# Projections and setup products spread between cross attention units, with a tanh gate and the final attention inside the feed-forward, in a transformer block with a second attention layer, on one core

## The chip, the cores and the metric

The kernel runs on 1 core of one Trainium2 chip, as one launch. The metric is the device time of that launch in microseconds, the median of a few runs. Its engines are TensorE (PE in the profile; PEld is its weight load), VectorE (DVE), ScalarE (ACT), GpSimd (POOL) and SyncE (SP, which here only issues DMAs).

## The reference

Input `x` is [2, 1024, 256], a context is [2, 77, 256]. Everything is fp32.

```
x  = x + attention1(ln1(x), ln1(x))          # 16 heads of 16, 1024 keys
x  = x + attention2(ln2(x), context)         # 16 heads of 16, 77 keys
h  = ln3(x) @ Wff1 + bff1                    # [., 2048]
lin, g = split(h)
x  = x + (lin * (g * sigmoid(1.702 * g))) @ Wff2 + bff2
# second layer: one head over the whole width of 256, 77 keys
Q, K, V = x Wq^T + bq, c Wk^T + bk, c Wv^T + bv
out = softmax(Q K^T / 16) V Wfc^T + bfc
x  = norm_w * rms_normalize(out + x)
```

The kernel never forms Q: it makes `g1 = Wq K^T`, `cb` (the part of the scores that comes from `bq`) and `vw = V Wfc^T + bfc` from the context and the weights once. These nine small products (two for K, two for V, two for `g1`, one for `cb`, two for `vw`) are called the setup products below.

## The kernel before

The program is written out by hand: each engine has its own stream, and semaphores join them. An engine runs its stream strictly in order, so that the place of a piece in the text is its place in time. Tokens are handled in 4 blocks of 512 (block 0 and 1 are batch 0), each of 4 tiles of 128; heads in 8 groups of 4 (groups 0 to 3 are batch 0). The stages:

- **Projections.** Block by block, layer norm, a transpose on PE (`turn`, L657), projections of q and k in two fp16 parts (`project`, L671; ACT makes the high part at L1142, DVE the remainder at L1489), which go to DRAM and come back in the layout that the score matmuls want. The keys' score maxima of group 0 begin here (`scores` L704, reduced by DVE in `reduce_tile`, L1497): 24 tiles of them before the first attention step. Between these tiles PE makes the products of the context (`setup`, L788), among them the nine setup products, which ACT copies out (L1202, L1204).
- **Self attention.** 8 groups of 16 steps; a step has four score matmuls (L856), four exponentials on ACT (L1246), the weighting (L868), and two tiles of maxima for the next group on DVE.
- **After self attention, batch 1.** `chain(0, 1)` is a generator of 17 pieces on each engine: two turns of the attended values, eight output products (L829) with the residual add (L1589) and layer norm on DVE, and for each of the blocks 2 and 3 a turn of the normalized rows (L657) and two projections to q of the cross attention (L671), and a last empty piece. `AHEAD` pieces run first, then pieces stand between the first tiles of cross scores (`FIRST_S2`, `scores_2`, L946), and the last three stand in cross group 0 (`pieces`).
- **Cross attention.** 8 groups of 8 units (`cross_unit`): a score matmul (L957), an exponential (L1304), and by unit number also a tile of maxima for the group after next (L946, reduced at L1686), the turn of the maxima (L982), the weighting (L965) and the turn of the result (L976). `chain(1, 0)`, the 12 pieces after cross attention of batch 0, stands in groups 5, 6 and 7.
- **Feed-forward.** 32 chunks (4 blocks of 8): `widen` (12 matmuls, L1033 to L1035, first the gate's bank, then the linear one), the gate on ACT with its bias (L1359), the product on DVE (`hidden`, L1734), a split in a high and low part (L1349 ACT, L1740 DVE), and three chunks later `narrow` (12 matmuls, L1048 to L1050). `chain(1, 1)` stands in the first eight chunks. For blocks 0 to 2 the turn of the finished rows and the scores of the final attention (L1063) follow in a later block.
- **Final attention.** After the last chunk: exponentials by tile with their sum (L1378), turns (L1072), copies (L1383), weighting (L1081), the residual (L1760), sums of squares (L1391), the root by 13 tiny DVE instructions a block (`root_steps`, L1447 to L1455), scaling on ACT (L1397) and on POOL (L614), for the last block on DVE (L1802), and stores.

```
TAIL = (1, 1, 1, 1, 1, 2, 1, 2, 1, 2, 2, 2)
AHEAD, FIRST_S2 = 6, (0, 1, 0, 1, 0, 1, 0, 1) * 2
def pieces(G, n):
    if G == 0:
        return 1 if n in (1, 3, 5) else 0
    return 1 if G >= GROUPS - 3 and n % 2 == 0 else 0
```

## Time and profile before

| | |
|---|---|
| median of 3 runs | 765.85 us (764.49 to 768.3) |
| the profiled execution, its time | 763.57 us |
| its span, first to last instruction | 761.1 us |
| mean granted TensorE clock | 0.943 |
| busy share of the span: PE, DVE, ACT, POOL | 90%, 72%, 66%, 9% |
| 512 exponentials of self attention on ACT | 312.8 us |

Times within the span count from its first instruction. The PEclk column of a stretch is the granted clock as a share of full speed: 1.00 is 2.4 GHz and 0.50 is 1.2 GHz. A matmul's busy time includes its way through the array, so the pace of a stream of matmuls is read from one start to the next.

### The profile page before, as it was taken

Reading aid. Unit: us, or ns where it says so; the run is one execution under the profiler, and the core shown is the slowest. Engines: PE = TensorE matmul, PEld = TensorE weight load, DVE = VectorE, ACT = ScalarE, POOL = GpSimd, SP = SyncE. Lnnn points to the kernel's source line nnn. Section 1 sums busy time; section 2 is a strip of 40 time slices with the busy share of each in tenths; the row PEclk is TensorE's granted clock in tenths of the full one; section 3 lists DMA queues with packets and bytes.
Section 4 is the critical chain, followed back from the end, with each engine's and each line's share of the span. In section 5 each row is a group of like instructions: output and inputs, shape, how many; then the busy total and the mean of one; then the engine's idle time right before and its main releaser. Section 6 shows DMA issues by size and latency. Waiting matters only on the chain.

```text
span 761.1 us, 11110 instructions
## 1 busy us (share of the span) xinstructions
PE 684.0 (90%) x4072; PEld 326.7 (43%) x4072; DVE 546.9 (72%) x954; ACT 501.5 (66%) x902; POOL 72.1 (9%) x85
## 2 busy tenths in 40 slices
PE   4989899999999999999999975899989999999981
PEld 2644422222222222222223342333547888888871
DVE  6678999999999999999973557544475954343367
ACT  2542499999999999999998731655664343233274
POOL 2080800000000000000000205100020110000004
PEclk9999999999999999999999997955788999999995
DMA  9456350202020100001000021211000000000003
GB/s 295 180 189 229 92 191 7 65 1 70 1 71 1 44 28 4 27 1 29 1 1 0 28 81 35 66 42 34 2 1 1 1 1 1 1 1 1 1 0 111
DMA packets 35113, 36.87 MB, mean 48 GB/s; under 512 B 6132, under 2 KB 28276, under 8 KB 34804
## 3 DMA queue, kind: packets, MB, share of 16 engines
q1 hardware_dynamic: 33904, 35.87, 14.8%
q8 instruction: 32, 0.52, 0.3%
q0 software_dynamic: 1024, 0.24, 0.3%
q14 instruction: 21, 0.17, 0.1%
q10 hardware_dynamic: 132, 0.07, 0.0%
HBM read 23.09 MB, written 12.74 MB: 47 GB/s over the span
## 4 chain that ended last, share of the span: by engine, by line
PE 70%; ACT 14%; DVE 10%; issue 5%; POOL 1%; ACTq 0%; DVEq 0%; POOLq 0%
PE ps L868 16%; PE ps L856 12%; ACT probs L1246 8%; PE ps L671 6%; PE ps L1033 4%; PE ps L1034 4%; PE ps L1035 4%; PE ps L829 3%; PE ps L965 3%; PE ps L657 3%; PE ps L704 2%; PE ps L957 2%; PE ps L976 2%; PE ps L1049 2%; PE ps L679 2%
## 5 line engine op out<-in xcount | busy, mean ns | idle before, releaser
L1246 ACT ACTIVATE probs<-ps,unfit 128x512 f32<-128x512 f32 x512 | 312.8, 693 | 21.5 <-PE ps L856 15.3
L1497 DVE TENSOR_REDUCE mm<-ps 128x2 f32<-128x1024 f32 x256 | 301.0, 1219 | 17.1 <-PE ps L704 9.6
L856 PE MATMUL ps<-stack 50*128 50x512 f16 x512 | 147.6, 384 | 11.6 <-ACT probs L1246 0.8
L868 PE MATMUL ps<-probs,v 128*32 128x512 f32 x1024 | 136.4, 604 | 2.7 <-ACT outT L1251 2.7
L856 PEld LDWEIGHTS ps<-stack 50*128 50x128 f16 x512 | 36.4, 93 | 191.1 <-ACT probs L1246 185.1
L704 PE MATMUL ps<-stack 48*128 48x512 f16 x512 | 105.6, 381 | 6.2 <-ACT mT L1191 4.5
L1359 ACT ACTIVATE early<-ps,cols 128x512 f32<-128x512 f32 x32 | 22.0, 687 | 88.4 <-PE ps L1035 88.4
L585 POOL TENSOR_TENSOR x<-x,rows 128x1024 f32<-128x1024 f32 x12 | 28.1, 2354 | 493.0 <-DVE tok L1478 492.9
L1734 DVE SCALAR_TENSOR_TENSOR hid<-ps,cols,early 128x512 f32<-128x512 f32 x32 | 24.0, 751 | 69.8 <-PE ps L1035 65.9
L1304 ACT ACTIVATE probs<-ps,unfit 96x512 f32<-96x512 f32 x64 | 42.3, 680 | 28.7 <-PE ps L957 28.5
L1033 PE MATMUL ps<-x_hi,wff_hi 128*128 128x512 f32 x128 | 52.0, 406 | 0.0
L1034 PE MATMUL ps<-x_lo,wff_hi 128*128 128x512 f32 x128 | 50.9, 398 | 0.0
L1035 PE MATMUL ps<-x_hi,wff_lo 128*128 128x512 f32 x128 | 50.4, 394 | 0.0
L1686 DVE TENSOR_REDUCE mm<-ps 128x8 f32<-128x616 f32 x32 | 25.5, 797 | 27.9 <-PE ps L946 27.8
L704 PEld LDWEIGHTS ps<-stack 48*128 48x128 f16 x512 | 25.7, 94 | 35.6 <-DVE mm L1497 10.4
L868 PEld LDWEIGHTS ps<-probs,v 128*32 128x32 f32 x1024 | 20.6, 107 | 37.3 <-issue 30.2
L1048 PE MATMUL ps<-wff_hi,hid_hi 128*128 128x256 f32 x128 | 36.5, 285 | 0.0
L1049 PE MATMUL ps<-wff_lo,hid_hi 128*128 128x256 f32 x128 | 36.1, 282 | 0.0
L829 PE MATMUL ps<-wo,wkv 128*128 128x256 f32 x128 | 33.6, 394 | 2.6 <-ACT wkv L1128 1.6
L1050 PE MATMUL ps<-wff_hi,hid_lo 128*128 128x256 f32 x128 | 35.8, 280 | 0.0
L1589 DVE TENSOR_TENSOR x<-ps,x 128x256 f32<-128x256 f32 x48 | 19.0, 418 | 23.3 <-PE ps L829 20.9
L1133 ACT ACTIVATE xT<-ps,cols 128x512 f32<-128x512 f32 x24 | 17.7, 778 | 25.1 <-PE ps L657 24.7
(164 smaller groups left out, 888.2 us busy)
## 6 DMA issues: line engine op xcount, KB each, us to landing
v_groups<-early SPq DMA_DIRECT2D x8, 512.0 KB, 3.1
stack<-q_parts SPq DMA_DIRECT2D x64, 64.0 KB, 2.0
v<-v_groups SPq DMA_DIRECT2D x8, 512.0 KB, 4.1
x<-in_x SPq DMA_DIRECT2D x4, 512.0 KB, 7.6
q_parts<-probs SPq DMA_DIRECT2D x8, 256.0 KB, 3.9
k_parts<-probs SPq DMA_DIRECT2D x8, 256.0 KB, 2.1
stack<-k_parts SPq DMA_DIRECT2D x16, 128.0 KB, 2.6
stack<-q_parts SPq DMA_DIRECT2D x64, 32.0 KB, 1.9
```

The lines of the kernel that those rows point to most:

```text
L671: mm_ = eng.matmul(ps[:, proj_bank(u), 0:n], w[:, c, P * o:P * o + P], src[:, c, c0:c0 + n], start=(c == 0), stop=(c == NC - 1))
L704: mm_ = eng.matmul(ps[:, 2 * s_slot(G, j, i) + tile, :], qs[rows_i, slot, half, q, P * t:P * t + P], stack[rows_i, SLOTS + slot, q, BLK * ...
L829: mm_ = eng.matmul(ps[:, out_bank(k), 0:D], attT[i // TPB][:, c, P * t:P * t + P], w[:, c, :], start=(c == 0), stop=(c == NC - 1))
L856: eng.matmul(ps[:, st_bank(n), :], stack[rows_of(tile, KROWS), SLOTS + slot, q, P * kc:P * kc + P], qs[rows_of(tile, KROWS), slot, half, q ...
L868: mm_ = eng.matmul(ps[32 * h:32 * h + 32, PV, :], v1[:, G % 2, kc, 32 * h:32 * h + 32], probs[:, k % 2, h, :], start=(kc == 0), stop=(kc = ...
L1033: eng.matmul(ps[:, bank, :], wh, xh[:, c, :], start=(c == 0), stop=False)
L1034: eng.matmul(ps[:, bank, :], wh, xl[:, c, :], start=False, stop=False)
L1035: mm_ = eng.matmul(ps[:, bank, :], wl, xh[:, c, :], start=False, stop=(c == NC - 1))
L1049: eng.matmul(out, hh, w2l, start=False, stop=False)
L1246: eng.activation(probs[:, k % 2, HEADS[h], :], ps[:, st_bank(n), :], ACT.Exp, scale=unfit[:, 0:1]).then_inc(exp_done, 1)
L1304: eng.activation(probs[0:CTXP, half, HEADS[h], :], ps[0:CTXP, ST + h % 2, :], ACT.Exp, scale=unfit[0:CTXP, 1:2]).then_inc(exp_done, 1)
L1497: eng.tensor_reduce(dst, ps[:, 2 * slot:2 * slot + 2, :], AX.X, ALU.max).then_inc(s_red, 1)
```

## The change

1. **Setup products.** The nine leave the projections stage. A generator `final_setup` on PE and DVE puts them in units (2,1), (2,3), (2,5), (3,0), (3,2), (3,4), (3,6), (4,1), (4,3) (group, unit) of cross attention. DVE copies them out, no longer ACT. 22 and no longer 24 tiles of maxima (`FIRST_TILES = 11` pairs) come before the first attention step; the last two stand inside that step. The turn of the first maxima stands after the 18th tile.
2. **Projections.** The four pieces of `chain(0, 1)` in the second half of `FIRST_S2`, and the three of group 0, now stand in groups 0 and 1, one to every second unit; `chain(1, 0)` begins one unit of work earlier, at the end of group 4. The fp16 parts of the cross q go to six slots in the space of the used keys, since their old place still holds weights. SP stores block 2's parts, loads group 4's first half, stores block 3's, and then loads the second half.
3. **Gate.** `g * sigmoid(1.702 g)` is computed as `(tanh(0.851 g) + 1) * (0.5 g)`: two activations on ACT (`Tanh` and `Identity`) and one more DVE instruction (`gated_half`) a chunk.
4. **Final attention.** For blocks 0 to 2 all of it is in the feed-forward's chunks; exponentials are one instruction a block after a subtraction of the maximum on DVE, and ACT and POOL no longer scale. Of block 2 the weighting and what follows is still at the end. For block 3 it goes by pairs of tiles: the last four chunks are narrowed tile by tile, so that the first two tiles finish earlier. The sum of the exponentials for block 3 comes from a column of ones in `vw`.

The diff's core:

```diff
-        AHEAD, FIRST_S2 = 6, (0, 1, 0, 1, 0, 1, 0, 1) * 2
+        AHEAD, FIRST_S2 = 6, (0, 1, 0, 1, 0, 1, 0, 1) + (0,) * 8
...
-            if G == 0:
-                return 1 if n in (1, 3, 5) else 0
-            return 1 if G >= GROUPS - 3 and n % 2 == 0 else 0
+            if G < len(PIECES_1):
+                return PIECES_1[G][n]
+            return PIECES_2[G - GROUPS // 2][n] if G >= GROUPS // 2 else 0
+
+        PIECES_1 = ((1, 0, 1, 0, 1, 0, 1, 0), (1, 0, 1, 0, 1, 0, 0, 0))
+        PIECES_2 = ((0, 0, 0, 0, 0, 0, 0, 1), (1, 0, 1, 0, 1, 0, 1, 0), (1, 0, 1, 0, 1, 0, 1, 0), (1, 0, 1, 0, 1, 0, 0, 0))
+        SETUP_UNITS = ((2, 1), (2, 3), (2, 5), (3, 0), (3, 2), (3, 4), (3, 6), (4, 1), (4, 3))
...
+            while first_scores:
+                tile_of_scores()
+                if len(first_scores) == 2 * FIRST_TILES - 18:
+                    eng.wait_ge(su_done, SETUP_1)
+                    eng.wait_ge(m_step, 3)
+                    eng.matmul(ps[0:96, MISC, 0:P], mpart[:, 0, :], identh[:, :], start=True, stop=True).then_inc(m_turned, 1)
...
                     cross_unit(G, n)
-                    advance(after_self if G == 0 else after_cross, pieces(G, n))
+                    if (G, n) in SETUP_UNITS:
+                        next(fillers)
+                    advance(after_self if G < GPB else after_cross, pieces(G, n))
...
-                eng.activation(gate[:, n % 2, :], ps[:, GATE, :], ACT.Gelu_apprx_sigmoid,
-                               bias=cols[:, i:i + 1]).then_inc(gate_done, 1)
+                eng.activation(gate[:, n % 2, :], ps[:, GATE, :], ACT.Tanh, scale=GELU / 2, bias=gate_cols[:, 0, f:f + 1])
+                eng.activation(half_gate[:, n % 2, :], ps[:, GATE, :], ACT.Identity, scale=0.5,
+                               bias=gate_cols[:, 1, f:f + 1]).then_inc(gate_done, 1)
...
+            def gated_half(n):
+                eng.wait_ge(gate_done, n + 1)
+                g = gate[:, n % 2, :]
+                eng.scalar_tensor_tensor(out=g, in0=g, scalar=1.0, in1=half_gate[:, n % 2, :], op0=ALU.add, op1=ALU.mult).then_inc(gated, 1)
...
+                if i == 4:
+                    l1_turn(blk)
+                if i == 5:
+                    l1_weigh(blk)
...
+            narrow_last(LAST_CHUNKS[0:3], (0, 1, 2))
+            l1_weigh(last - 1)
+            narrow_last(LAST_CHUNKS[3:4], (0, 1, 2))
+            narrow_last(LAST_CHUNKS[0:2], (3,))
+            last_turn(0)
+            narrow_last(LAST_CHUNKS[2:4], (3,))
+            last_scores(0)
+            last_turn(1)
+            last_scores(1)
+            last_turn_probs(0)
+            last_weigh(0)
+            last_turn_probs(1)
+            last_weigh(1)
```

How the streams move, at three places (line numbers are each kernel's own).

PE at the start of cross attention, before: L946 is a tile of cross maxima, L982 the turn of the maxima, L671 a projection, L657 a turn of rows, L957 the first unit's score matmul.

```order
L657 MATMUL ps<-ident,tok 128x128 x8
L946 MATMUL ps<-k,stack 128x78 x8
L982 MATMUL ps<-identh,mpart 96x128
L671 MATMUL ps<-xT,wq 128x512 x2
L946 MATMUL ps<-k,stack 128x78 x8
L671 MATMUL ps<-xT,wq 128x512 x2
L946 MATMUL ps<-k,stack 128x78 x8
L657 MATMUL ps<-ident,tok 128x128 x8
L957 MATMUL ps<-stack,k 96x512
```

The same place in the changed kernel, where L992 is the tile of maxima, L1028 its turn, L1003 the unit's score matmul, L678 a turn and L692 a projection.

```order
L992 MATMUL ps<-k,stack 128x78 x16
L1028 MATMUL ps<-identh,mpart 96x128
L992 MATMUL ps<-k,stack 128x78 x16
L1003 MATMUL ps<-stack,k 96x512
L992 MATMUL ps<-k,stack 128x78 x8
L678 MATMUL ps<-ident,tok 128x128 x8
L1003 MATMUL ps<-stack,k 96x512 x2
L992 MATMUL ps<-k,stack 128x78 x8
L1028 MATMUL ps<-identh,mpart 96x128
L692 MATMUL ps<-xT,wq 128x512 x2
```

Two turns and two projections no longer stand before the first unit, but behind it.

DVE in a chunk in the middle of the feed-forward, before:

```order
L1734 SCALAR_TENSOR_TENSOR hid<-ps,cols,early 128x512
L1740 TENSOR_TENSOR hid_lo<-hid,hid_hi 128x512
L1677 TENSOR_TENSOR x_lo<-xT,x_hi_56 128x2x512
L1734 SCALAR_TENSOR_TENSOR hid<-ps,cols,early 128x512
L1740 TENSOR_TENSOR hid_lo<-hid,hid_hi 128x512
```

and in the changed kernel, where L1867 is `gated_half`, L1877 `hidden`, L1883 the low part, L1560 and L1563 steps of the root, and L1922 the last scaling of a finished block:

```order
L1883 TENSOR_TENSOR hid_lo<-hid,hid_hi 128x512
L1560 TENSOR_TENSOR ms<-rms 128x4
L1560 TENSOR_TENSOR ms<-ms,half_ms 128x4
L1563 SCALAR_TENSOR_TENSOR rms<-ms,rms 128x4
L1560 TENSOR_TENSOR ms<-rms 128x4
L1560 TENSOR_TENSOR ms<-ms,half_ms 128x4
L1563 SCALAR_TENSOR_TENSOR rms<-ms,rms 128x4
L1867 SCALAR_TENSOR_TENSOR early<-early 128x512
L1877 SCALAR_TENSOR_TENSOR hid<-ps,cols,early 128x512
L1811 TENSOR_TENSOR x_lo<-xT,x_hi_56 128x2x512
L1922 SCALAR_TENSOR_TENSOR x<-x,rms,rows 128x256 x4
L1883 TENSOR_TENSOR hid_lo<-hid,hid_hi 128x512
```

A chunk has one long DVE instruction more, and in some chunks the work of the final attention.

PE from the end of the last chunk on, before (L1072 turns the probabilities, L657 the rows, L1081 weights, L1063 makes scores):

```order
L1050 MATMUL ps<-wff_hi,hid_lo 128x256
L1072 MATMUL ps<-ident,probs 77x128 x8
L657 MATMUL ps<-ident,x 128x128 x8
L1081 MATMUL ps<-vw,p1T 128x256 x4
L1063 MATMUL ps<-g,xT 128x77 x8
L1072 MATMUL ps<-ident,probs 77x128 x4
L1081 MATMUL ps<-vw,p1T 128x256 x8
L1072 MATMUL ps<-ident,probs 77x128 x4
L1081 MATMUL ps<-vw,p1T 128x256 x4
```

and now (L1157 turns rows, L1167 makes scores, L1176 turns probabilities, L1185 weights):

```order
L1095 MATMUL ps<-wff_hi,hid_lo 128x256
L1167 MATMUL ps<-g,xT 128x77 x4
L1157 MATMUL ps<-ident,x 128x128 x4
L1167 MATMUL ps<-g,xT 128x77 x4
L1176 MATMUL ps<-ident,probs 77x128 x2
L1185 MATMUL ps<-vw,p1T 128x257 x2
L1176 MATMUL ps<-ident,probs 77x128 x2
L1185 MATMUL ps<-vw,p1T 128x257 x2
```

What was three blocks and a fourth is now the fourth alone, in two halves.

## Rows read from the trace of the kernel before

**Rows 1.** The page: granted TensorE clock in 40 slices; the gate's group
```profile
PEclk9999999999999999999999997955788999999995
...
L1359 ACT ACTIVATE early<-ps,cols 128x512 f32<-128x512 f32 x32 | 22.0, 687 | 88.4 <-PE ps L1035 88.4
```

**Rows 2.** Busy time by stretch: us of each engine (instructions), PEclk, DMA share, GB/s
```profile
462.00:473.00 11.00, 6.11 (x23) 3.10 (x23) 7.05 (x24) 1.82 (x3) 5.47 (x5) 0.53 0.01 3
473.00:493.00 20.00, 16.90 (x135) 7.41 (x135) 11.90 (x19) 13.51 (x24) 5.07 (x6) 1.00 0.20 64
493.00:541.00 48.00, 45.89 (x266) 19.23 (x267) 18.94 (x39) 25.29 (x45) 0.00 (x0) 0.50 0.11 31
541.00:565.00 24.00, 22.52 (x137) 11.25 (x133) 17.31 (x62) 17.25 (x30) 2.36 (x1) 1.00 0.01 2
...
592.00:606.00 14.00, 13.14 (x75) 11.36 (x74) 13.41 (x37) 4.40 (x7) 2.37 (x1) 1.00 0.01 2
606.00:723.60 117.60, 117.60 (x704) 103.73 (x703) 50.45 (x96) 39.42 (x64) 2.40 (x1) 1.00 0.00 1
```

**Rows 3.** Timeline, end of the projections: start, us, engine, line, [idle before]
```profile
79.33 8.00 DVE L1497 TENSOR_REDUCE mm<-ps 128x2 f32<-128x1024 f32 x7
...
90.01 4.15 ACT L1246 ACTIVATE probs<-ps,unfit 128x512 f32<-128x512 f32 x7 [0.56 <-PE ps L856]
...
90.16 9.44 DVE L1497 TENSOR_REDUCE mm<-ps 128x2 f32<-128x1024 f32 x8 [1.45 <-PE ps L704]
```

**Rows 4.** Timeline, end of the stage between the attentions
```profile
466.68 1.38 DVE L1478 TENSOR_SCALAR tok<-x,mv,rstd 128x256 f32<-128x256 f32 x4
...
469.33 3.73 PE L671 MATMUL ps<-xT,wq 128*128 128x512 f32 x4
...
473.23 1.98 PE L671 MATMUL ps<-xT,wq 128*128 128x512 f32 x4
...
477.98 0.41 PE L957 MATMUL ps<-stack,k 50*96 50x512 f16 x1
```

**Rows 5.** Chain of waits, two setup products: start, us, what
```profile
84.42 0.72 PE ps L788 x4
...
87.44 1.61 PE ps L788 x6
```

**Rows 6.** Timeline of PE, cross attention: weightings, turns of maxima, one turn of rows
```profile
484.62 1.06 PE L965 MATMUL ps<-probs,v 96*32 96x512 f32 x8
...
492.99 1.54 PE L965 MATMUL ps<-probs,v 96*32 96x512 f32 x8
...
501.15 0.34 PE L982 MATMUL ps<-identh,mpart 128*96 128x128 f16 x1
...
524.94 0.34 PE L982 MATMUL ps<-identh,mpart 128*96 128x128 f16 x1
...
538.67 1.91 PE L657 MATMUL ps<-ident,tok 128*128 128x128 f32 x8
```

**Rows 7.** Timeline of DVE, one chunk of block 2
```profile
655.59 0.75 DVE L1734 SCALAR_TENSOR_TENSOR hid<-ps,cols,early 128x512 f32<-128x512 f32 x1 [2.84 <-PE ps L1035]
656.26 0.68 DVE L1740 TENSOR_TENSOR hid_lo<-hid,hid_hi 128x512 fp32r<-128x512 f32 x1
```

**Rows 8.** Groups by line after 723.6: busy us, mean ns, idle before
```profile
L1391 ACT ACTIVATE sq<-x 128x256 f32<-128x256 f32 x16 | 6.6, 413 | 1.1
...
L1391 ACT ACTIVATION_READ_ACCUMULATOR sq<-x 128x1 f32 x16 | 3.0, 187 | 0.0
```

**Rows 9.** Timeline after the last chunk's widening
```profile
729.19 1.04 PE L1072 MATMUL ps<-ident,probs 128*77 128x128 f32 x8
...
743.59 0.65 DVE L1452 TENSOR_TENSOR ms<-ms,half_ms 128x4 f32<-128x4 f32 x1
...
755.81 0.16 DVE L1455 SCALAR_TENSOR_TENSOR rms<-ms,rms 128x4 f32<-128x4 f32 x1
756.01 1.67 DVE L1802 SCALAR_TENSOR_TENSOR x<-x,rms,rows 128x256 f32<-128x256 f32 x4
```

More of the change, by code:

```diff
@@ L787, in setup @@
                 for i, (lhs, rhs) in enumerate(terms):
-                    mm_ = eng.matmul(ps[0:m, 6 + k % 2, 0:n], lhs, rhs, start=(i == 0), stop=(i == len(terms) - 1))
+                    mm_ = eng.matmul(ps[0:m, bank, 0:n], lhs, rhs, start=(i == 0), stop=(i == len(terms) - 1))
                 mm_.then_inc(su_full, 1)
-                tile_of_scores()
-            eng.wait_ge(w_in["wl1"], 64)
             cut = [slice(CTX * b, CTX * b + CTX) for b in range(B)]
             for b in range(B):
-                setup(CTX, D, [(ctxT[:, c, cut[b]], wkv2[:, c, D:2 * D]) for c in range(NC)])
@@ L1084, in _, with last_weigh @@
+            def last_weigh(p):
+                eng.wait_ge(l_pT, last + p + 1)
+                if p == 0:
+                    eng.wait_ge(l_y, TPB * last)
+                for t in range(2 * p, 2 * p + 2):
+                    eng.matmul(ps[:, LAST_W[p] + t % 2, 0:D + 1], p1T[0:CTXP, last, P * t:P * t + P],
+                               vw[0:CTXP, last // 2, :], start=True, stop=True).then_inc(l_pv, 1)
             eng.wait_ge(exp_done, 72 * GROUPS)
@@ L1417, in _ @@
+            hid_high(FC * BLOCKS - 1)
+            last_copy(0)
+            l1_squares(last - 1, (0, 1))
+            last_copy(1)
+            l1_squares(last - 1, (2, 3))
+            last_exps(0)
+            last_exps(1)
+            last_turn_copy(0)
+            last_turn_copy(1)
+            l1_squares(last, range(TPB))
         @block.vector
@@ L1632, in step @@
                     attended(2 * G, 2 * turn_slot(G, k))
+                if G == 0 and k == 0:
+                    for i in range(2):
+                        reduce_tile(G, FIRST_TILES, i)
                 if lead < GROUPS:
@@ new lines, in _, with last_max, last_residual @@
+            last = BLOCKS - 1
+            def last_max(p):
+                tiles = slice(2 * p, 2 * p + 2)
+                less_max(last + p, s1[:, last, tiles, :], ps[:, LAST_S[p], 0:2 * CTX].rearrange("p (t n) -> p t n", t=2),
+                         m1[:, last, tiles], [P, 2, CTX], last // 2)
+            def last_residual(p):
+                n, bank = TPB * last + 2 * p, LAST_W[p]
+                eng.wait_ge(l_pv, n + 2)
+                link(eng.reciprocal(r1[:, last, 2 * p:2 * p + 2], ps[:, bank:bank + 2, D]))
+                for t in range(2):
+                    eng.scalar_tensor_tensor(out=x[:, n + t, :], in0=ps[:, bank + t, 0:D], scalar=r1[:, last, 2 * p + t:2 * p + t + 1],
+                                             in1=x[:, n + t, :], op0=ALU.mult, op1=ALU.add).then_inc(l_y, 1)
@@ new lines, in steps_of @@
+            def steps_of(chain, n):
+                for _ in range(n):
+                    next(chain, None)
+            after_cross = chain(1, 1)
+            root = iter(())
+            for n in range(FC * BLOCKS):
+                blk, i = final_step(n)
+                if n >= 1:
+                    hid_low(n - 1)
+                if i == 0 and blk >= 1:
+                    root = l1_root(blk - 1)
+                    steps_of(root, 6)
+                if i == 1 and blk >= 1:
+                    steps_of(root, 7)
+                if i == 4:
+                    l1_sum(blk)
+                gated_half(n)
+                hidden(n)
@@ new lines, in _ @@
+            hid_low(FC * BLOCKS - 1)
+            l1_residual(last - 1, (0, 1))
+            for t in range(2):
+                add(2, TPB * last + t)
+            l1_residual(last - 1, (2, 3))
+            for t in range(2, TPB):
+                add(2, TPB * last + t)
+            root = l1_root(last - 1)
+            last_max(0)
+            steps_of(root, 6)
+            last_max(1)
+            steps_of(root, 7)
+            last_residual(0)
+            l1_scale(last - 1, (0, 1), l_out)
@@ L1807 @@
+            last_residual(1)
+            l1_scale(last - 1, (2, 3), l_out)
+            for _ in l1_root(last):
+                pass
+            l1_scale(last, range(TPB), l_last)
 def kernel(**inputs):
```

479 lines of the change are left out of this document (266 added, 213 removed).

## The prediction

> **What bounds the kernel now.** I read the page's slices first: PE is busy nearly everywhere, so a stage is mostly worth what its PE stream lasts, but the granted clock has a dip in the third quarter [rows 1]. The windows by stage come next [rows 2]. In 462 to 473 PE is busy 6.1 of 11 us at a clock of 0.53: the engines wait there. In 493 to 541 PE is busy 45.9 of 48 us, all of it at 0.50 (1.2 GHz): 48 us of cross attention at the lower level, though PE hardly rests. From 606 to 723.6 PE has no gap. After 723.6, where the last chunk's widening ends, another 37.4 us pass to the end of the span: a tail of short instructions that wait for each other [rows 8, 9]. The timelines of the four places show what ends each wait.
>
> At the start of self attention DVE decides: its reductions of maxima run one behind the other from 79.33, at 1.14 us each (8.00 for 7), while the first exponential starts at 90.01, and DVE itself then idles 1.45 us before the 25th tile [rows 3]. Between the attentions the layer norm on DVE ends at 468.06 (466.68 + 1.38), then two projections and a turn pass through PE, ACT and DVE before the first unit's matmul at 477.98 [rows 4].
>
> **The change, part by part.**
>
> *Start of self attention.* Nine products leave PE and 24 tiles become 22. The last reduction of 22 ends 2 x 1.14 = 2.3 us earlier, so the first exponential could start 4 to 5 us sooner, but every step then wants two tiles from a DVE that still owes two. DVE loses its idle 1.45 us, and ACT, which paces the plain steps, makes up the rest only if PE's order lets it. Bounds: 0 (DVE-paced, and later slack eats it) and 5 (ACT keeps its whole lead). I take **2.5 us** gained, a little above DVE's own 1.6 to 2.3, being nearest to it.
>
> *Before the first cross unit.* What is left behind the layer norm at 468.06 is three tiles of maxima, for each of which I allow 1.2 us through PE and DVE, and the turn of the maxima with its DMA. That ends near 472, and the unit starts there, not at 477.98 [rows 4]: **6.0 us** gained. The clock had fallen before 473 [rows 2] and PE now does less there, so the units begin at the lower level. Before, it was back at 473, after the projection of 3.73 us at 469.33. Now a turn stands behind unit 0 and a projection behind unit 2; I charge **3.0 us** lost (about 6 us of PE work at half speed until then), with bounds of 1 and 8.
>
> *Work that moves into the units.* Two turns at 1.0 and two projections at 2.0 [rows 4, 9] are 6.0 us; seven setup products at 0.9 and two at 1.6 [rows 5] are 9.5 us. In all **15.5 us** of PE work, on a PE that is the bound here. ACT is busy 25.3 of 48 us and DVE 18.9 in that stretch [rows 2], so DVE's nine copies (about 0.35 us each) hide. ACT loses them.
>
> *The clock in the units.* Two groups from one turn of maxima to that of two groups later take 23.8 us at the lower level, 11.9 a group [rows 6]. At the full level a group without pieces between, from one weighting to the third, takes 8.4 us (484.62 to 492.99) with some 1.2 us of gaps on PE, so 7.2 of work; a piece in the gaps fills them partly, I allow 0.5 a group. Four groups ran at the lower level. If the clock stays at full, they give back 4 x (11.9 - 7.2) = 18.8, less 2.0 for what gaps stay: **16.8 us** gained. Why it should stay: before, it fell in group 1, after the last projection and with only narrow work behind it, and was back in group 5 behind two turns (1.91 us at 538.67) [rows 6]; from 541 to 565, with a piece in every second unit, it stood at 1.00 [rows 2]. The new order puts a piece in nearly every second unit of groups 0 to 7. The longest stretches without one are the end of group 1 and three units of group 4, shorter than what it survived before it fell.
>
> The Trainium skill's page TensorE: Matmul & The Clock Gate, in the section on the clock gate ("What's actually happening"), says that the gate follows how busy PE has recently been. By that, units at 96% busy would have been at the full level, and pieces that raise 96% to 100% would change nothing; here the trace disagrees with its 48 us at 0.50. By that rule the 16.8 us would not come from the pieces, and the outcome would be the first rival's.
>
> *Feed-forward.* A chunk lasts 4.19 us on PE (DVE: 2.84 idle, then 0.67 and 0.68) [rows 7]. DVE gets a third instruction of 0.68 to 0.75, so 2.1 of 4.19; ACT a second activation, about 0.6, so 1.9. The path gate bank, tanh 0.69 (as the gate's activation now [rows 1]), identity 0.6, `gated_half` 0.7, `hidden` 0.75 and semaphores is 3.0 us, and the linear bank is wanted again 4.2 us after the gate's end: 1 us to spare, so nothing, if it stays there. In the first eight chunks DVE is busy 13.4 of 14 us with layer norm [rows 2]; there 0.7 us more in three or four chunks lands on the path: **2.5 us** lost, bounds 0 and 6. Final attention inside the chunks puts two turns of 0.45 and two weightings of 1.0 on PE: **2.9 us** lost. DVE's share of it, per block 4 scalings and 4 residuals at 0.42, 13 root steps at 0.2 and the maxima, is 9 us on some 20 us of idle in eight chunks; hidden. The setup of tanh needs no load of a table between exponentials and gate, which I book at nothing at the start.
>
> *Tail.* Before: 37.4 us. After, from the last widening, at the pace of the last 48 matmuls of `narrow`, from 723.6 to 729.19 [rows 9], 0.117 each: a turn 0.45, 36 of them 4.2, weighting 1.0, six more 0.7: 6.4. Turn and copy of the first pair of tiles, 1.3: 7.7. Scores 0.9, second turn 0.5, its copy behind two squares (0.60 each [rows 8]): 9.9; scores: 10.9. DVE: six root steps wait for the squares of block 2 (11.1): 12.4, maxima 1.0: 13.4. Exponential 0.45, copy 0.5, weighting 0.9: 15.2. Two residual pairs of 1.1 and two scalings of 0.85: 19.3. Root 13 x 0.2 (0.16 busy [rows 9]): 21.9. Four scalings 1.7 [rows 9]: 23.6. The output's transfer took 3.4 us before (757.7 to the end): 27.0. Part of it is that POOL is silent: beside POOL's scaling a root step took 0.65 us, without it 0.16 [rows 9]. **10.4 us** gained, bounds 7 and 13.
>
> *Sum*: 2.5 + 6.0 - 3.0 - 15.5 + 16.8 - 2.5 - 2.9 + 10.4 = 11.8 us gained. The profiled execution took 763.57 us (span 761.1), so the forecast is 751.8, rounded to **752 us**. The median of the runs shown, 765.85, lies 2.3 us above that execution; I do not add it.
>
> **The rivals.**
>
> *The clock stays at the lower level among the pieces.* The units' own work does not hold the clock, and small pieces (0.9 us in two units) may not either. Then each of four groups costs 11.9 as before plus its pieces at half speed: the 16.8 us are not gained and the 15.5 us double, so 32 us worse than the forecast: 784 us, slower. For it: the half level lasted 48 us with PE 96% busy [rows 2], and the stage now begins low. Against it: two turns ended it. A group at the lower level costs 4.2 + 3.9 = 8.1 us, so it decides from about two groups on (11.8 + 3.8 lost); one such group gives 760.
>
> *DVE and ACT become the bound of the chunks.* If the spare 1 us is gone, because a wait is longer than the busy times or pieces of final attention stand before `gated_half`, each chunk slips. At 0.4 us in 24 chunks that is 10 us: 762 us, no change. For it: four engines' hops in series where there were three; DVE's 96% in the first block [rows 2]. Against it: 2.84 us of idle DVE in each chunk [rows 7].
>
> *A transfer is late.* Group 4's second half of q is loaded only after block 3's projections, now in group 1; the store, its landing and four loads take some 8 us from there, and group 4's maxima want it in the middle of group 2, about as late. Two or three us, 755; in the range.
>
> **How the numbers follow.** A measurement of this kernel tells differences over 0.5%, 3.8 us. Forecast with the clock held, 744 to 758 with its terms' bounds: 0.72. The clock lost for about one group, or the late transfer with it, 757 to 762: 0.12. The chunks slip, 759 to 767: 0.08, half of it over 762. The clock lost for two groups or more, 768 to 785: 0.08. The range 744 to 762 leaves 0.12 at the upper side and some at the lower. Faster 0.87, same 0.06, slower 0.07.
>
> **What would show it.** Right: a granted clock of 1.00 from soon after the first unit to the feed-forward; the first unit's matmul some 8 us earlier; units of about 10 to 11 us a group with PE over 90% busy; PE without gaps in blocks 1 to 3; 27 us from the last widening to the end. Wrong: 0.50 in groups 2 to 4; PE waiting for DVE's product or ACT's gate in most chunks; the first exponential earlier but group 1 of self attention not; a tail where ACT's squares or DVE's root are preceded by idle time over 2 us.

## The result, and the profile after

| | before | changed kernel |
|---|---|---|
| median | 765.84 us (764.49 to 768.3, 4 runs) | 756.86 us (756.29 to 758.41, 4 runs) |
| profiled execution, its time / span | 763.57 / 761.1 us | 756.29 / 754.5 us |
| mean granted clock | 0.943 | 0.954 |

The ratio is 0.9892 (95% interval 0.9852 to 0.9932): faster by about 1.1%, over the 0.5% that a measurement of this kernel can tell. The forecast was 752 us, 4.9 us below the median. Compared as gains, the medians lie 9.0 us apart and the two profiled spans 6.6 us, where 11.8 us were forecast.

The kernel before has a wide spread of its own: of 19 later executions of it, five took 757.9 to 758.5 us at a mean granted clock of 0.949 and the others 761.1 to 768.1 us at 0.931 to 0.943, so that its best executions, of which no trace was kept, come close to the changed kernel's 756.3 to 758.4.

The granted clock on the page, in slices of 18.9 us:

```profile
PEclk9999699999999999999999997899968999999996
```

The dip of [rows 1] is nearly gone from the third quarter; what is left lies at its two ends, and a new dip stands in the fifth slice, at the start of self attention. The windows that answer to [rows 2] (busy time of each engine, granted clock, DMA share, GB/s):

```profile
462.00:473.00 11.00, 2.94 (x36) 1.85 (x37) 8.53 (x28) 0.93 (x2) 5.46 (x5) 0.50 0.01 3
473.00:493.00 20.00, 18.34 (x115) 8.40 (x113) 8.39 (x15) 13.68 (x25) 4.38 (x5) 0.89 0.16 51
493.00:541.00 48.00, 45.52 (x378) 23.73 (x378) 29.74 (x74) 31.89 (x58) 0.00 (x0) 1.00 0.13 37
...
552.00:570.00 18.00, 14.74 (x51) 8.10 (x52) 7.44 (x20) 8.68 (x14) 2.35 (x1) 0.53 0.01 1
```

From 493 to 541 PE is as busy as before (45.5 of 48 us against 45.9), but at 1.00 and not at 0.50. With more work in them the units are shorter. But the level falls again before the feed-forward: 0.53 from 552 to 570.

To place the rest, I cut both executions at the same instructions. On ACT these are copies of turned maxima (L1300, L1391), on DVE the first, ninth and last `hidden` (L1877). For the changed kernel, from the timeline:

```profile
100.50 0.25 ACT L1300 ACTIVATE mT<-ps 32x128 f16<-32x128 f32 x1
...
468.75 0.27 ACT L1391 ACTIVATE mT<-ps 64x128 f16<-64x128 f32 x1 [22.41 <-PE ps L1028]
479.60 0.26 ACT L1391 ACTIVATE mT<-ps 64x128 f16<-64x128 f32 x1
541.53 0.26 ACT L1391 ACTIVATE mT<-ps 64x128 f16<-64x128 f32 x1
...
570.36 0.75 DVE L1877 SCALAR_TENSOR_TENSOR hid<-ps,cols,early 128x512 f32<-128x512 f32 x1
618.71 0.75 DVE L1877 SCALAR_TENSOR_TENSOR hid<-ps,cols,early 128x512 f32<-128x512 f32 x1
727.45 0.75 DVE L1877 SCALAR_TENSOR_TENSOR hid<-ps,cols,early 128x512 f32<-128x512 f32 x1
```

The differences of these starts, and of the same instructions in every other kernel of this study, make one table (us; the last column is the span's end less the last `hidden`):

| kernel | start to A | A to B | B to C | C to D | D to E | E to chunk 0 | 0 to 8 | 8 to 31 | tail |
|---|---|---|---|---|---|---|---|---|---|
| before | 103.1 | 296.8 | 69.6 | 13.3 | 68.7 | 26.4 | 41.4 | 104.3 | 37.4 |
| changed | 100.5 | 296.9 | 71.3 | 10.9 | 61.9 | 28.8 | 48.4 | 108.7 | 27.0 |
| e1 tanh alone | 103.0 | 297.0 | 69.7 | 13.2 | 73.3 | 26.5 | 48.3 | 104.4 | 36.2 |
| e2 spread alone | 102.7 | 297.0 | 69.6 | 10.8 | 67.9 | 29.2 | 42.0 | 104.3 | 37.4 |
| e3 no gated_half | 100.5 | 296.9 | 69.7 | 10.2 | 61.9 | 28.5 | 43.3 | 108.7 | 27.5 |
| e4 setup back | 100.8 | 296.9 | 71.3 | 10.9 | 67.9 | 29.2 | 46.4 | 108.8 | 27.0 |
| e5 fill start | 101.1 | 296.9 | 69.7 | 11.5 | 61.9 | 29.1 | 48.3 | 108.8 | 27.0 |
| e6 fill cross | 103.3 | 296.9 | 76.4 | 9.8 | 61.9 | 28.8 | 48.1 | 108.8 | 27.0 |
| e7 old gate first | 101.5 | 296.9 | 69.7 | 11.0 | 61.9 | 28.9 | 43.3 | 108.8 | 26.0 |
| e8 w1 early | 103.6 | 296.9 | 69.7 | 11.0 | 62.2 | 28.8 | 44.5 | 108.8 | 27.0 |
| e9 POOL in four | 104.0 | 296.9 | 68.4 | 10.0 | 61.9 | 28.8 | 47.3 | 108.8 | 27.0 |
| e10 all three | 104.2 | 296.9 | 68.4 | 10.0 | 62.2 | 28.0 | 41.5 | 108.8 | 27.0 |
| e11 and order | 100.5 | 296.9 | 68.4 | 10.8 | 62.2 | 28.7 | 41.9 | 108.8 | 27.0 |
| e12 half fill | 103.7 | 297.0 | 69.5 | 11.0 | 61.9 | 28.9 | 48.3 | 108.8 | 27.0 |

A and B are the second and the sixteenth copy, in the steady part of self attention; C, D and E belong to cross groups 0, 1 and 7.

Three things in it are no part of the change: they differ between executions of the same instructions. I call them draws.

- **The first column.** The changed kernel, e3, e6 to e8 and e12 have the same streams up to A and reach it between 100.5 and 103.7 us (e9 to e11, which differ there by POOL's addition alone, between 100.5 and 104.2). The first projection, at 14 us, runs at one clock level or the other: it took 1.96 us at 13.96 in the changed kernel and 3.75 at 14.04 in the kernel before, and e1, e6, e8 to e10 and e12 drew 3.75 again. A part of the rest goes with how long the lower level then lasts behind 79 us: to 92 in the changed kernel, to 95 in e7, whose A is at 101.5.
- **B to C.** The changed kernel's clock was 0.64 from 432 to 436, while e3, the same program up to the feed-forward, stood at 1.00 there. This costs 1.7 us (71.3 against the 69.6 or 69.7 of seven other kernels; e4 drew it too).
- **The first block.** In the changed kernel the clock is at 0.50 from 610.6 to 614.0 us. The eighth chunk, from `hidden` to `hidden`, takes 6.5 us; in e4, with the same chunks and the clock at 1.00, it takes 4.9. e1, e5, e6, e9 and e12 have such a stretch as well, the other kernels have none.

The last one matters most, since it lies in the stage where the forecast went wrong. Whole first block (chunk 0 to 8), of the kernel before, the changed one, e4 and e10; columns as in the windows above:

```profile
578.02:619.41 41.39, 39.79 (x215) 33.84 (x215) 31.43 (x78) 18.56 (x31) 4.77 (x2) 1.00 0.00 1
...
570.36:618.71 48.35, 43.34 (x228) 36.35 (x227) 37.18 (x87) 23.32 (x38) 5.74 (x2) 0.96 0.00 1
...
577.02:623.40 46.38, 41.69 (x228) 34.94 (x227) 37.17 (x87) 23.21 (x38) 5.73 (x2) 1.00 0.00 1
...
569.79:611.30 41.51, 40.77 (x228) 35.18 (x227) 27.49 (x75) 16.82 (x26) 6.94 (x8) 1.00 0.00 1
```

The eight intervals between one `hidden` and the next (us):

| kernel | 1 | 2 | 3 | 4 | 5 | 6 | 7 | 8 |
|---|---|---|---|---|---|---|---|---|
| before | 3.1 | 5.5 | 4.5 | 7.5 | 6.1 | 7.1 | 3.2 | 4.3 |
| changed | 4.4 | 5.5 | 4.9 | 10.3 | 5.5 | 7.9 | 3.4 | 6.5 |
| e4 setup back | 4.4 | 5.5 | 4.5 | 10.3 | 5.5 | 7.9 | 3.4 | 4.9 |
| e3 no gated_half | 3.8 | 5.6 | 4.8 | 9.5 | 4.7 | 7.1 | 2.9 | 4.9 |
| e7 old gate first | 3.7 | 5.5 | 4.5 | 9.5 | 4.7 | 7.1 | 2.8 | 5.5 |
| e8 w1 early | 4.3 | 5.5 | 4.5 | 9.7 | 4.9 | 7.3 | 3.4 | 4.9 |
| e10 all three | 3.7 | 5.5 | 4.5 | 7.5 | 4.5 | 6.7 | 3.4 | 5.8 |

### The profile page after: what moved, and what is told of

Same layout as the page of the kernel before. It is cut to its first block and busy times, and to the rows that moved or that the text cites. A ratio compares the mean times of both kernels' runs of the same rounds, so it can differ in the third digit from the quotient of the medians.

```text
span 754.5 us, 11157 instructions
## 1 busy us (share of the span) xinstructions
PE 671.8 (89%) x4072; PEld 321.6 (43%) x4072; DVE 574.1 (76%) x1014; ACT 508.9 (67%) x887; POOL 65.0 (9%) x74
## 5 line engine op out<-in xcount | busy, mean ns | idle before, releaser
L894 PE MATMUL ps<-stack 50*128 50x512 f16 x512 | 149.2, 389 | 10.8 <-ACT probs L1336 0.4
L725 PE MATMUL ps<-stack 48*128 48x512 f16 x512 | 107.8, 390 | 10.2 <-DVE mm L1605 5.2
L612 POOL TENSOR_TENSOR x<-x,rows 128x1024 f32<-128x1024 f32 x12 | 29.1, 2438 | 491.1 <-DVE tok L1586 491.0
L1867 DVE SCALAR_TENSOR_TENSOR early<-early 128x512 f32<-128x512 f32 x32 | 22.1, 691 | 34.4 <-ACT early L1453 34.4
L1452 ACT ACTIVATE early<-ps,gate_cols 128x512 f32<-128x512 f32 x32 | 22.0, 688 | 37.7 <-PE ps L1084 37.7
L1444 ACT ACTIVATE hid_hi<-hid 128x512 fp32r<-128x512 f32 x32 | 20.2, 632 | 39.0 <-DVE hid L1877 39.0
L1093 PE MATMUL ps<-wff_hi,hid_hi 128*128 128x256 f32 x128 | 38.1, 298 | 0.0
L1094 PE MATMUL ps<-wff_lo,hid_hi 128*128 128x256 f32 x128 | 36.2, 283 | 0.0
L1820 DVE TENSOR_REDUCE mm<-ps 128x8 f32<-128x616 f32 x32 | 25.5, 797 | 12.1 <-PE ps L992 11.5
```

What stands on the lines that cost most here:

```text
L725: mm_ = eng.matmul(ps[:, 2 * s_slot(G, j, i) + tile, :], qs[rows_i, slot, half, q, P * t:P * t + P], stack[rows_i, SLOTS + slot, q, BLK * ...
L894: eng.matmul(ps[:, st_bank(n), :], stack[rows_of(tile, KROWS), SLOTS + slot, q, P * kc:P * kc + P], qs[rows_of(tile, KROWS), slot, half, q ...
L1093: eng.matmul(out, hh, w2h, start=(f == 0), stop=False)
L1094: eng.matmul(out, hh, w2l, start=False, stop=False)
```

## The experiments

Before them my theory was: the spread pieces, the nine small products above all, hold the clock in the units; and the missing 5 us lie in the first feed-forward block, where DVE was full and I priced `gated_half` too low. Rivals: the clock would hold without the products; the block is late for another reason. The changed kernel was timed in the first series alone, so a difference to its 756.86 us is one between series; the kernel before had medians of 765.8, 765.8, 766.4 and 765.7 us in the four series.

**e1, the tanh gate alone.** The kernel before, with

```diff
-                eng.activation(gate[:, n % 2, :], ps[:, GATE, :], ACT.Gelu_apprx_sigmoid,
-                               bias=cols[:, i:i + 1]).then_inc(gate_done, 1)
+                eng.activation(gate[:, n % 2, :], ps[:, GATE, :], ACT.Tanh, scale=GELU / 2, bias=gate_cols[:, 0, f:f + 1])
+                eng.activation(half_gate[:, n % 2, :], ps[:, GATE, :], ACT.Identity, scale=0.5,
+                               bias=gate_cols[:, 1, f:f + 1]).then_inc(gate_done, 1)
...
+                eng.scalar_tensor_tensor(out=g, in0=g, scalar=1.0, in1=half_gate[:, n % 2, :], op0=ALU.add, op1=ALU.mult).then_inc(gated, 1)
```

> The kernel before with the tanh gate alone: two activations and the product gated_half per chunk, final attention and projections where they were. Theory A (DVE is the bound of the first feed-forward block and pays for gated_half there, 0.69 us a chunk): the first eight chunks take 5 to 8 us longer than before, the other 24 as long as before or up to 2 us longer, the whole kernel 5 to 10 us slower, 771 to 776. Rival B (the first block's 7 us of the changed kernel come from what stands at the block's start there, the earlier end of cross attention and its clock): the first block grows by under 3 us, and the kernel by under 3.

770.75 us (769.08 to 773.45, 4 runs), ratio to before 1.0117 (1.0054 to 1.018). The first eight chunks took 48.3 us instead of 41.4, chunks 8 to 31 104.4 instead of 104.3. So the gate alone costs 6.9 us in the profiled execution, all of it in the first block; theory A, though the medians are only 4.9 us apart. A stretch at 0.50 like the changed kernel's, from 623.0 to 626.4, is in these 6.9 us. In the other 24 chunks the gate is free. (The 4.6 us more from D to E are a longer stay at the lower clock level, to 551.3 and not 541.2, in units that this edit does not touch.)

**e2, the spread projections alone**, with the setup products left at the start:

```diff
-        AHEAD, FIRST_S2 = 6, (0, 1, 0, 1, 0, 1, 0, 1) * 2
+        AHEAD, FIRST_S2 = 6, (0, 1, 0, 1, 0, 1, 0, 1) + (0,) * 8
...
+        PIECES_1 = ((1, 0, 1, 0, 1, 0, 1, 0), (1, 0, 1, 0, 1, 0, 0, 0))
```

> The kernel before with the projections spread over cross units alone; the nine setup products stay at the start, so that groups 2, 3 and most of 4 have no piece between their units. Theory A (the nine small products are what holds the clock there): the granted clock falls to 0.50 again within groups 2 to 4, these take about 12 us each, and the kernel gains 3 to 6 us on before: 760 to 763. Rival B (the pieces in groups 0 and 1, or no fall in the beginning, are enough and the bare units keep the clock): 1.00 through groups 1 to 7, groups 2 and 3 at 8.4 us each, and the kernel gains 15 to 20 us: 746 to 751.

762.61 us (760.83 to 763.66, 10 runs), ratio 0.9996 (0.9959 to 1.0032), taken over the 19 executions of the kernel before with their wide spread: not to be told from it. The windows of e2 show why:

```profile
493.00:503.00 10.00, 8.83 (x78) 3.67 (x78) 6.47 (x14) 7.38 (x15) 0.00 (x0) 0.93 0.24 70
503.00:529.00 26.00, 24.84 (x149) 9.35 (x142) 10.19 (x21) 13.03 (x23) 0.00 (x0) 0.50 0.17 40
```

The last projection of group 1 ends at 491.74; the clock falls between 501 and 502 and comes back between 532 and 533, behind the two turns at 528.80 and 532.42, though PE was 96% busy between. What C to D gains (2.6 us) and D to E (0.8) comes back as 2.8 in E to chunk 0, where the lower level now lasts from 559.7 to 576.8 (before: 565.1 to 575.4).

**e4, the setup products back**, from the other side: the changed kernel with

```diff
-        SETUP_UNITS = ((2, 1), (2, 3), (2, 5), (3, 0), (3, 2), (3, 4), (3, 6), (4, 1), (4, 3))
+        SETUP_UNITS = ()
-        SETUP_1, SETUP_2 = B, 9
-        FIRST_TILES = 11
+        SETUP_1, SETUP_2 = 6, 5
+        FIRST_TILES = 12
```

and the products between the first score tiles as before.

> The changed kernel with its nine setup products at their old place between the first score tiles (24 tiles first, not 22). Theory A (the products hold the clock in groups 2 to 4): the clock falls to 0.50 there, PE's 9.5 us of work gone from the units but about 14 us added by the level, 758 to 763. Rival B (bare units keep the level once they have it): clock 1.00, 9.5 us of PE's work gone from the bound stage; the start pays 0 to 2.5 for them: 747 to 750, faster than the changed kernel.

761.39 us (760.84 to 764.84, 10 runs), 4.5 above the changed kernel. Its windows are those of e2 again:

```profile
503.00:529.00 26.00, 24.85 (x146) 9.55 (x143) 10.39 (x21) 13.22 (x24) 0.00 (x0) 0.50 0.15 40
```

The changed kernel has nine more products in these units (priced at 9.5 us; from start to next start they take 8.1 there) and is still 6.0 us shorter from D to E. That is theory A: the spreading of the projections is not enough, in either kernel, and with the products in groups 2 to 4 the clock holds. e4's clock falls between 501 and 502. PE's timeline of the changed kernel has two of the products just before, and a third at 503.24:

```profile
498.34 0.79 PE L807 MATMUL ps<-ctxT,early 128*128 128x154 f32 x4
...
500.08 0.79 PE L807 MATMUL ps<-ctxT,early 128*128 128x154 f32 x4
```

At the start the products' leaving gained hardly anything: 100.5 against 100.8 to A.

**e3, gated_half left out.** The changed kernel with the instruction replaced by its semaphore's increment; it leaves out (tanh + 1) * half, so that the gate is the tanh alone.

```diff
-                eng.scalar_tensor_tensor(out=g, in0=g, scalar=1.0, in1=half_gate[:, n % 2, :], op0=ALU.add, op1=ALU.mult).then_inc(gated, 1)
+                eng.sem_inc(gated, 1)
```

> The changed kernel without the DVE instruction gated_half (this leaves (tanh + 1) * half out; the gate is the tanh alone). Theory A (it is this instruction on a full DVE that cost the first block some 7 us where 2.5 were forecast, and the later blocks 1 to 2): 6 to 9 us faster than the changed kernel, 748 to 751, nearly all of it before chunk 8. Rival B (ACT's second activation and the four hops from bank to hidden are what delays a chunk): under 3 us faster.

749.14 us (749.09 to 751.03, 4 runs), 7.7 less than the changed kernel. Of the 7.2 us between the two profiled spans 5.0 are the first block (48.4 to 43.3), nothing is chunks 8 to 31 (108.7 both), 1.7 is the draw at 432, 0.7 is C to D and 0.3 E to chunk 0; the tail is 0.5 longer. But 1.6 of the 5.0 is the eighth chunk, which has no stretch at 0.50 here. Against e4, which has none either, the instruction is worth 3.1 us (46.4 to 43.3): 0.5 to 0.8 in each of the chunks 1 and 4 to 7, which is about its 0.69, and nothing in the other three. So the mechanism of theory A holds, at half its size; 1.9 us of the block's 7.0 remain without the instruction.

**e5, PE kept busy at the start**, with

```diff
+            def keep(n):
+                for _ in range(n):
+                    eng.matmul(ps[:, PV, 0:D], wkv2[:, 0, 0:P], wkv2[:, 0, D:2 * D], start=True, stop=True)
...
             while first_scores:
                 tile_of_scores()
+                keep(2)
```

and four more pairs in the first step.

> The changed kernel with idle-time products (128x128 by 256 columns, into a bank that nobody reads yet) on PE behind each of the last score tiles and within the first step of self attention, where its granted clock was 0.50 from 79 to 92 us. They change no result. Theory A (the nine setup products held the clock there; without them weighting and scores run at half speed and eat what their leaving gained): clock 1.00 throughout, the steady copies of turned maxima 1.5 to 2.5 us earlier, 754 to 756. Rival B (DVE's maxima pace the stretch, whatever PE's clock): the clock holds, but no copy comes earlier: within 0.5 us of the changed kernel.

758.0 us (756.23 to 758.99, 4 runs), beside 756.86; A at 101.1 instead of 100.5. The window 78 to 92 of e5 (the changed kernel has 0.51 there):

```profile
78.00:92.00 14.00, 14.00 (x72) 6.75 (x72) 12.24 (x12) 4.48 (x8) 14.00 (x28) 1.00 0.49 125
```

The clock held and nothing was gained, as B says. It is not a clean verdict: with PE full, DVE waited 0.15 to 0.38 us for PE before each of five reductions, 1.6 us in all, so a gain of up to that much may be hidden behind the filling's own cost. And a longer stay at the lower level does cost: in e7, with the same early first projection, it lasts to 94.8 and not 91.8, DVE waits 0.92 us more for PE before a tile at 95.63, and A comes 1.0 us later.

**e6 and e12, PE kept busy before the first cross unit**: `keep(28)` and `keep(14)` behind the maxima at 459.

> The changed kernel with 28 such products (about 7.5 us) on PE while it waits for the layer norm before the first cross unit, 460 to 468 us, where the clock falls to 0.50 until 478. Theory A (my charge of 3.0 us for initial units at the lower level is real): clock 1.00 from 460, the feed-forward's first product 2 to 4 us earlier, 753 to 755. Rival B (the first units wait for the turned maxima's DMA, DVE and ACT, so that PE's level there costs little): under 1 us.

> The changed kernel with 14 idle-time products before the first cross unit, since 28 took 15.3 us and ran past the layer norm by 8. They should end near 467.5. If the lower level in the first units costs what I charged (3.0 us), 2 to 3 us faster than the changed kernel; if e6's reading holds (1.0 us from one turn of maxima to the next, nothing after it), within 1 us; the granted clock should be 1.00 from 468 on in both cases, unless half of the products does not bring it back, and then nothing changes.

e6 took 760.66 us (758.19 to 762.97, 4 runs), slower: I had mis-sized the filling, whose 28 products ran 15.3 us and past the layer norm, B to C 76.4. Behind them the first unit, at 479.49, began at 1.00, but the clock was at 0.50 again from 480.5 to 483.9. C to D was 9.8 instead of 10.9, while D to E and what follows stayed as they were. e12, with half of it, took 757.03 us (756.01 to 757.92, 4 runs), no difference. Its window behind 473:

```profile
473.00:478.00 5.00, 5.00 (x30) 3.42 (x31) 2.51 (x5) 3.38 (x5) 4.57 (x7) 0.50 0.00 0
```

The expected 1.00 from 468 on did not last: the filling, over at 467.46, held the clock until 472.4, just before the first unit's matmul at 472.98. PE had done 1.2 us of work between. Then it was at 0.50 until 479.2, with PE busy throughout. So e12 only moved the dip's start to a place where PE waits anyway.

What the lower level costs in the first units is read from all kernels together. It comes back at a different distance behind C in each (us; found by cutting the windows finer):

| | e9 | e10 | e3 | e2 | e11 | changed | e4 | e8 | e7 | e12 | e5 |
|---|---|---|---|---|---|---|---|---|---|---|---|
| level back, behind C | 7.0 | 7.0 | 7.4 | 8.5 | 8.6 | 8.7 | 8.8 | 8.9 | 9.0 | 9.1 | 10.1 |
| C to D | 10.0 | 10.0 | 10.2 | 10.8 | 10.8 | 10.9 | 10.9 | 11.0 | 11.0 | 11.0 | 11.5 |

Each us at the lower level makes C to D 0.5 us longer, as for work on PE alone that runs at half speed. The first unit starts 2.9 us behind C, so the changed kernel has 5.8 us of units at the lower level, which by this slope cost 2.9 us (an estimate). By the same slope e6, with 3.4 us of it left, should need 9.7; it took 9.8. So I had charged the 3.0 rightly, and e6 shows 1.0 only because it took away less than half of the level.

**e7, the old gate in the first eight chunks, e8, the weights' splits early, e9, POOL's addition in four, and e10, all three**, each on the changed kernel.

```diff
+                if n < FC:
+                    eng.activation(gate[:, n % 2, :], ps[:, GATE, :], ACT.Gelu_apprx_sigmoid,
+                                   bias=cols[:, COL_FF + FC + f:COL_FF + FC + f + 1]).then_inc(gate_done, 1)
+                    return
```

```diff
+        W1_UNITS = ((3, 5), (4, 1), (4, 5), (5, 1), (5, 5), (6, 1), (6, 5), (7, 1))
...
+                    if (G, n) in W1_UNITS:
+                        w1_low(W1_UNITS.index((G, n)))
...
-                if n + 2 < FC:
-                    w1_low(n + 2)
```

```diff
-                    eng.tensor_tensor(xb, xb, rows[:, row:row + 1, :].to_broadcast([P, TPB, D]), ALU.add).then_inc(bias_added, 1)
+                    for t in range(TPB):
+                        ins = eng.tensor_tensor(xb[:, t, :], xb[:, t, :], rows[:, row, :], ALU.add)
+                    ins.then_inc(bias_added, 1)
```

> The changed kernel with the one-instruction gate of before in the first eight chunks, and the tanh gate from chunk 8 on, where the first final attention begins. Theory A (what the first block lost, 7 us, is the tanh gate alone: 5 us of gated_half on a full DVE and 2 of ACT's second activation): the first block takes 41 to 42 us as before, 749 to 751. Rival B (ACT has to load another table twice and the block's start is held by weights and layer norm): the first block is 2 to 4 us shorter, 753 to 755.

> The changed kernel with the eight splits of the widening weights (an ACT copy and a DVE subtraction of 0.68 us each) taken out of the first chunks and done in cross groups 3 to 7, where both engines idle half the time. Theory A (DVE is what bounds the first block; 0.7 us a chunk less on it shortens a chunk by about that): first block 4 to 6 us shorter, cross attention as long as before, 751 to 753. Rival B (the block waits for the chain of layer norm, turn and projection, or the units get longer by as much): within 1.5 us of the changed kernel.

> The changed kernel with POOL's addition of the bias rows cut from one instruction of 128x1024 (2.34 us) a block into four of 128x256. Theory A (a DVE instruction that starts while POOL's runs, and reads only SBUF, ends only with it: hid_lo 2.75 us instead of 0.68 at 591.95, mpart 2.34 instead of 0.17 at 459.64): hid_lo there falls to about 1.3, mpart to under 1, and with them 1.2 to 1.5 us each of DVE's path to the fifth chunk and to the first cross unit: 753.5 to 755. Rival B (DVE waits for each of the four in turn, or the stall was not on the path): within 0.5 us of the changed kernel.

> The changed kernel with three things together: the old gate in the first eight chunks, the splits of the widening weights in cross groups 3 to 7, and POOL's addition in four. Theory A (the first block is bound by the sum of DVE's work, so the gains add up): first block 37 to 39 us, 745 to 748. Rival B (with DVE relieved, the block is bound by the chain of layer norm, turns and output projection of the last two token blocks): first block about 41, 749 to 750.

e7: 750.74 us (749.75 to 752.99, 4 runs), 6.1 less than the changed kernel; first block 43.3, 3.1 us less than e4's. Theory A in its total, though the block stops 1.9 us short of the 41.4 of before, just as e3 did. ACT loads another table twice (1.28 us each, at 564.51 and 640.19), and no stage is longer for it: chunks 8 to 31 take 108.8, and the tail ran 26.0.

e8: 754.35 us (753.69 to 755.2, 4 runs); first block 44.5, 3.8 shorter than the changed kernel's, for 0.2 in the units. 1.6 of that is again the eighth chunk without its stretch at 0.50; against e4 it is 1.9, some 0.6 in each of the chunks 4 to 6, about what a split takes on DVE (0.68). So in these chunks DVE's work counts nearly in full, whichever of the two instructions is taken from it. The forecast of 4 to 6 was too high.

e9: 754.52 us (751.09 to 755.09, 4 runs). What it was built on stands in the changed kernel's timeline, DVE and POOL at 591:

```profile
591.95 2.75 DVE L1883 TENSOR_TENSOR hid_lo<-hid,hid_hi 128x512 fp32r<-128x512 f32 x1
...
591.78 2.38 POOL L612 TENSOR_TENSOR x<-x,rows 128x1024 f32<-128x1024 f32 x1 [35.24 <-DVE tok L1586]
```

`hid_lo` takes 0.68 elsewhere; started 0.17 us behind POOL's addition, it ends 0.54 us after it. In e9:

```profile
461.47 0.72 DVE L1615 SCALAR_TENSOR_TENSOR mpart<-mm,mpart 128x32 f16<-128x32 f32 x1
...
591.26 1.10 DVE L1885 TENSOR_TENSOR hid_lo<-hid,hid_hi 128x512 fp32r<-128x512 f32 x1
```

Against the usual 69.6 to 69.7, B to C is 1.2 shorter and the first block, with its stretch at 0.50, 1.1: theory A. C to D is 0.9 shorter by the level alone, which comes back sooner.

e10: 749.42 us (746.83 to 750.72, 5 runs), ratio to before 0.9778 (0.9755 to 0.9802). It beats both kernels, with 7.4 us less than the changed one. But the first block took 41.5 us, not 37 to 39. The gains of 5.1, 3.8 and 1.1 do not add up to 10 but to 6.9; a part of that is a count taken twice, since e7 and e8 both lost the stretch at 0.50. From e4 on they are 3.1, 1.9 and 1.1, together 6.1, and 4.9 came. Theory A falls here, and rival B's 41 is what came, but not for B's reason: in the window above PE is busy 40.8 of e10's 41.5 us and DVE 27.5. What bounds the block now is PE's own work. It was nearly so in the kernel before, with PE at 39.8 of 41.4.

**e11, hid_low behind hidden again**, on e10:

```diff
                 hidden(n)
+                if 1 <= n < FC:
+                    hid_low(n - 1)
```

> The one before it, with hid_low of the chunk before placed behind hidden in the first eight chunks, as in the kernel before the change. Theory A (hid_low ahead of hidden puts 0.68 us, and what POOL stretches it to, between linear bank and hidden): 1 to 2 us faster than e10. Rival B (narrow waits for hid_low as soon as PE for hidden, so that one delay takes the place of the other): no difference, or slower by under 1 us.

751.62 us (747.07 to 752.64, 5 runs), first block 41.9 against 41.5. Rival B: the order does nothing once DVE is relieved. Whether it makes the 1.9 us that e3 and e7 lack was not tried without the other two edits, and stays open. They lie in the fourth chunk, 9.5 us against 7.5 before, where `hid_lo` takes 2.75 us beside POOL's addition; the fifth gives 1.4 of it back.

## Why the prediction was right, and where it was short

The direction, the range and the mechanism of the cross attention were right; the forecast was 4.9 us low, and the largest part of it is one mis-sized term, the first block. By the prediction's own terms:

- **Start of self attention, +2.5: measured about +0.3.** A came 2.6 us earlier, but e4, which has all nine products at the start and drew the same early first projection, reaches A at 100.8 against 100.5. With the later first projection the changed streams (e6, e8, e12) reach A at 103.3 to 103.7 and the old ones (before, e1) at 103.1 and 103.0, so there the products' leaving gains nothing. The bound 0 that I named (paced by DVE, eaten later) was the right end. I had not seen that PE without the products would fall to 0.50 from 79 to 92; e5 found no gain in undoing that, e7 a cost of 1.0 us where it lasts longer.
- **Before the first cross unit, +6.0: measured +5.5.** From C to the first unit's matmul it is 2.9 us (468.75 to 471.65) instead of 8.4 (469.57 to 477.98).
- **Initial units at the lower level, -3.0: about -2.9**, an estimate from the slope of 0.5 us per us over eleven kernels. The level came back at 477.5, after 5.8 us of units, as I took it to.
- **Moved work -15.5 and the clock +16.8: right in kind.** From the first unit's matmul to chunk 0 the kernel before took 100.0 us and the changed one 98.7: 1.3 gained, where the last three terms together say 1.7 lost. It hides two things of different sign. Up to E 3.7 us were gained; from E to chunk 0 2.4 were lost (28.8 against 26.4), where the level is at 0.50 from 552.6 to 569.7 and before was from 565.1 to 575.4. I had no term for that, and my sign of being right, 1.00 up to the feed-forward, did not come. I had credited the clock to turns, projections and products alike; e2 and e4 show that in groups 2 to 4 it takes the products.
- **First block, -2.5: measured -7.0.** This is the term that was mis-sized. I had the right row, DVE busy 13.4 of 14 us [rows 2], and then priced `gated_half` for three or four chunks. e4, with the same chunks, loses 5.0 us (46.4 against 41.4): of the 7.0, 1.6 is the stretch at 0.50, which I did not foresee, and 0.4 another draw, in the third chunk. Of the 5.0, `gated_half` is 3.1 by e3 against e4, at nearly its full 0.69 in five chunks; for the other 1.9 no experiment names one cause. And that row is one window: over the whole block PE was busier than DVE before the change, 39.8 and 31.4 of 41.4 us. My bound of 6 was too near for an execution with such a stretch.
- **Final attention on PE, -2.9: measured -4.4.** I took four matmuls of a weighting where a block has eight. The kernel before had the row for all eight, 3.60 us at half the clock, so 1.8; with the turn of probabilities at 0.45 that is 2.2 a block for two blocks, 4.4. With DVE's new work here fully hidden (e3: 108.7 with and without), PE sets the pace as forecast.
- **Tail, +10.4: measured +10.3**, 27.0 us from the last `hidden`'s start. The steps inside differ: four matmuls of the last weighting took 2.08 us at 740.89, at the lower level, where I had 0.9, and a root step 0.16 us busy as before.

The measured terms make 0.3 + 5.5 + 1.3 - 7.0 - 4.4 + 10.3 = 6.0; the draws of the two executions add 2.3 at the start and take 1.7 at 432, and the sum is 6.6, the difference of the spans.

Of the rivals, the one on the clock did not come, but e2 and e4 show how near it was: without nine small products it is what happens for 26 us, and e4 is 4.5 us slower than the changed kernel by it (6.0 more in the units, less the 2.0 by which its first block is shorter). The Trainium skill (TensorE: Matmul & The Clock Gate, "What's actually happening") says that the gate follows how busy PE has recently been. This case's windows do not agree: PE at 96% and 0.50 in e2's and e4's windows, 95% and 1.00 in the changed kernel's. How busy PE is doesn't tell these windows apart; what is in them does. The second rival, chunks bound by DVE and ACT, was real in some chunks of the first block and absent from the others. The late transfer left no trace: D to E is 61.9 or 62.2 in all kernels with the products.

## What to carry over

Price an added instruction at its full time on the engine that bounds the stage, and at nothing where that engine idles: here the same 0.69 us cost 0.5 to 0.8 us in five chunks and nothing in the 27 others. So choose a form by stage, as e7 does. And read the granted clock by stage before counting PE's work: a stage that sits at the lower level can take in more work and get shorter, if the level comes back with that work. And before two kernels' stages are compared, compare the clock in them: the stretch at 0.50 from 610.6 to 614.0 put 1.6 us on the account of an instruction that is worth 3.1.

## What was not expected of the hardware

- PE at 1.2 GHz while hardly ever idle, and kept at 2.4 with other work added: the units' own matmuls, mostly of 48 or 50 rows or 32 columns, and turns of 128x128 by 128 (e2, 503 to 529: 0.50, 24.84 of 26 us busy), and the same with fp32 products, most of 128x128 by 154, between them (493 to 541: 1.00, 45.52 of 48). Whether it is their shape, their type or their length that counts is not shown: no run put other work in their place in these groups.
- DVE instructions that read two tensors from SBUF can be held up by POOL. One on 128x32 took 2.34 us beside POOL's 128x1024 addition, and 0.72 behind one of 128x256; `hid_lo` 2.75 and 1.10. It is not every one, and not one way: at 608.05 `gated_half` took its 0.68 us inside POOL's addition of 607.61, which then took 3.36 us and not 2.34. Reductions that read PSUM were not held up: 0.80 us at 468.48, within POOL's 467.31 to 469.65.

```profile
459.60 2.34 POOL L612 TENSOR_TENSOR x<-x,rows 128x1024 f32<-128x1024 f32 x1 [32.42 <-DVE tok L1586]
459.64 2.34 DVE L1613 SCALAR_TENSOR_TENSOR mpart<-mm,mpart 128x32 f16<-128x32 f32 x1
```

The Trainium skill (GPSIMD Engine Reference, "Key points") states that GpSimd shares its SBUF interfaces with VectorE, with contention for DVE instructions that have two SBUF inputs. These rows agree: the two held instructions ended with POOL's (461.98 and 461.94) or 0.54 us after it (594.70 and 594.16).
